# Attention blocks three half steps apart, silu of the gate ahead of the scan's end, first gate means earlier

## The reference, cut to what matters

```python
# 1  x += tanh(g0) * mamba(ctx, z=layernorm(x))
x = silu(conv(in_proj @ ctx) + b);  dt = softplus(dt_proj @ low(x) + b)
state = state * exp(dt * A[:, n]) + (dt * x) * B[n]      # n = 0..15, along 512 tokens
y = (sum_n state * C[n] + D * x) * silu(z)
# 2  x += tanh(.) * bitlinear(gelu(bitlinear(layernorm(x), w1)), w2)   ternary weights, 8 bit rows
# 3  attention = softmax(q @ k.T), q and k from ctx alone;  x += tanh(.) * layernorm(x) @ attention.T
# 4  x += tanh(.) * (gelu(layernorm(x) @ p1 + b1) @ p2 + b2)            512 to 2048 to 512
```

## Time and profile before

| | |
|---|---|
| median of 3 runs | 1008.52 us |
| the profiled execution | 1010.51 us, span 1008.7 us |
| busy: PE, DVE, ACT, POOL | 823.4, 806.3, 684.1, 560.5 us |
| granted clock of TensorE, mean | 0.91 |
| scans end (last product, DVE) | 168, 396, 614 and 833 us |
| tail on PE | 915.1 to 1003.3 us |

### The profile page before, as it was taken

One profiled execution on the slowest core, in us unless ns is written; L12 is line 12 of the kernel. 1 busy time (PEld: TensorE's weight loads), 2 busy tenths in 40 slices (PEclk: granted clock), 3 DMA queues, 4 the chain that ended last, 5 costly groups with the idle time before them and its releaser, 6 DMA issues. The chain is left out here.

```text
span 1008.7 us, 9403 instructions
## 1 busy us (share of the span) xinstructions
PE 823.4 (82%) x2758; PEld 405.3 (40%) x2798; DVE 806.3 (80%) x937; ACT 684.1 (68%) x1004; POOL 560.5 (56%) x477
## 2 busy tenths in 40 slices
PE   6531244699699998899699989898799989898998
PEld 2210012344344444444344434444343434446887
DVE  4989986686999998887999997977999997653333
ACT  4678985877389975575599863765699855624442
POOL 0398795123798984233998882225998871232000
PEclk9755556798999999999999999999999999998999
DMA  8078994000179987111199966301499972200331
GB/s 289 0 134 191 268 210 94 1 1 3 41 156 233 228 197 187 52 54 42 29 198 239 236 135 166 105 1 42 87 220 212 226 153 84 105 1 22 104 105 63
DMA packets 47971, 123.76 MB, mean 123 GB/s; under 512 B 5920, under 2 KB 7072, under 8 KB 47408
## 3 DMA queue, kind: packets, MB, share of 16 engines
q0 software_dynamic: 17280, 62.92, 33.1%
q1 hardware_dynamic: 30640, 60.24, 17.9%
HBM read 56.03 MB, written 4.19 MB: 60 GB/s over the span
## 5 line engine op out<-in xcount | busy, mean ns | idle before, releaser
L1686 POOL TENSOR_TENSOR work<-du,bcast 128x1024 f32<-128x1024 f32 x128 | 358.4, 2859 | 43.5 <-ACT ccast L857 37.7
L1258 DVE TENSOR_TENSOR_SCAN pair<-pair,work 128x512 f32<-128x512 f32 x256 | 299.2, 1214 | 18.5 <-ACT pair L872 13.7
L872 ACT ACTIVATE pair<-dt,a_neg 128x512 f32<-128x512 f32 x256 | 165.7, 680 | 47.6 <-DVE work L1263 39.3
L642 PE MATMUL bank<-stage,ring 128*128 128x512 f32 x384 | 172.9, 593 | 2.5 <-ACT stage L1101 2.0
L1263 DVE TENSOR_TENSOR work<-pair,ccast 128x1024 f32<-128x1024 f32 x128 | 156.8, 1225 | 12.8 <-DVE pair L1258 0.5
L1697 POOL DMA_DIRECT2D u<-work x120 | 138.5, 1157 | 43.7 <-DMA u<-work 21.9
L435 PE MATMUL bank<-xd,pick 128*128 128x512 bf16 x108 | 48.1, 446 | 95.9 <-ACT bcast L857 70.2
L642 PEld LDWEIGHTS bank<-stage,ring 128*128 128x128 f32 x384 | 71.8, 190 | 80.9 <-issue 70.9
L656 PE MATMUL bank<-ring,stage 128*128 128x512 f32 x192 | 86.1, 594 | 1.7 <-ACT hx L1136 1.7
L435 PEld LDWEIGHTS bank<-xd,pick 128*128 128x128 bf16 x128 | 12.9, 101 | 152.6 <-ACT bcast L857 104.2
L531 PE MATMUL pair<-w1q,qT 128*128 128x512 bf16 x247 | 59.8, 389 | 10.4 <-ACT qT L1079 6.7
(11 more groups left out here) (181 smaller groups left out, 1562.2 us busy)
## 6 DMA issues: line engine op xcount, KB each, us to landing
u<-work POOLq DMA_DIRECT2D x120, 512.0 KB, 6.0
ring<-ffn_dram SPq DMA_DIRECT2D x120, 256.0 KB, 4.9
ring<-ffn_dram SPq DMA_DIRECT2D x16, 512.0 KB, 3.4
xres<-x_dram SPq DMA_DIRECT2D x4, 1024.0 KB, 5.4
stage<-w_dram SPq DMA_DIRECT2D x1, 4096.0 KB, 17.5
stage<-w_dram SPq DMA_DIRECT2D x4, 1024.0 KB, 8.1
out_dram<-stage SPq DMA_DIRECT2D x16, 256.0 KB, 2.1
ctxT<-ctxT_dram SPq DMA_DIRECT2D x4, 512.0 KB, 6.2
```

Source lines behind the costliest of these rows:

```text
L642: last = pe.matmul(banks[2 + f % 2][:], piece(b, f)[:, k * P:(k + 1) * P], xnT[:, k, :], start=k == 0, stop=k == J - 1)
L872: act.activation(pairs[s % DECAYBUFS][:, q, :], dt[:, p * HALF + q, :], ACT.Exp, scale=a_neg[:, p * HALF + q, n:n + 1]).then_inc(s_decay, 1)
L1258: dve.tensor_tensor_scan(pair[:, q, :], pair[:, q, :], rows[:, q, :], 0.0, ALU.mult, ALU.add).then_inc(s_scan, 1)
L1686: pool.tensor_tensor(work[:, s % SCANBUFS, :, :], du[:, p * HALF:(p + 1) * HALF, :], bcast[:, n % 2, :].unsqueeze(1).broadcast_to([P, HALF ...
```

## The change

The attention's slots become steps of the scan: block j has its product, maximum and exponentials at half step 19 + 3j, reciprocal and scaling one later, transposes and copy one later still. The last block is then copied at half step 30, and nothing of the attention is left behind the scan. DVE's reciprocal moves in between the two scans of a half step and its product. `FFN_DOWN` now has 14 pairs in slots 9 to 12 (eight of round 0, six of round 1) instead of 13; the one more is the pair with which the turning began.

For batch 0, the gate means move to slot 6, and the weight steps on ACT are dealt out again: four instead of six are left behind the scan. POOL's part for w2 (`weight_rms(1)`) moves from slot 11 to slot 10.

In `turning`, `first_turning`, `between` and `closing` a few steps change places, and `closing` has two new rows of eight matmuls ahead of the tail.

```diff
-ATT_SLOTS = {9: 0, 10: 1, 11: 2, 12: 3}
+ATT_FIRST, ATT_EVERY = 18, 3
+ZSTAT_FIRST = 6
-W_MEAN = {6: 0, 11: 1}
+W_MEAN = {6: 0, 10: 1}
...
-W_LATE = (("scale", 1, 1), ("sign", 1, 1), ("scale", 1, 2), ("sign", 1, 2), ("scale", 1, 3), ("sign", 1, 3))
+W_LATE = (("scale", 1, 2), ("sign", 1, 2), ("scale", 1, 3), ("sign", 1, 3))
...
+def att_step(slot, which, p, step):
+    n = state_at(slot, which)
+    if n is None or 2 * n + p < ATT_FIRST + step:
+        return None
+    j, rest = divmod(2 * n + p - ATT_FIRST - step, ATT_EVERY)
+    return j if rest == 0 and j < J else None
@@ PE
+            def attention(b, slot, which, p):
+                done = att_step(slot, which, p, ATT_EVERY)
+                if done is not None:
+                    att_transpose(b, done)
+                j = att_step(slot, which, p, 1)
+                if j is not None:
+                    energies(b, j)
...
             def first_turning(m):
-                keep_awake(16)
+                keep_awake(24)
                 gate_transposes(m, (0, 1, 2, 3))
...
             def turning(b, m):
-                f_pair(b, 1, 10)
                 gate_transposes(m, (0,))
                 gate_transposes(m, (1,))
+                f_pair(b, 1, 12)
                 gate_transposes(m, (2,))
-                f_pair(b, 1, 12)
                 f_pair(b, 1, 14)
...
                 q_transposes(m, (2,))
+                up1(m, 1, (FC - 1,))
                 q_transposes(m, (3,))
-                up1(m, 1, (FC - 1,))
@@ between
+                transpose_h(b, 1)
                 down1(b, 0)
-                transpose_h(b, 1)
...
-                scan_bcast(m, 0, 0)
                 attend(b, 0)
                 attend(b, 1, m)
+                scan_bcast(m, 0, 0)
@@ closing
                 attend(b, 0)
+                down1(b, 3)
                 norm_transpose(b, 2)
-                down1(b, 3)
                 attend(b, 1)
+                norm_transpose(b, 3)
                 attend(b, 2)
-                norm_transpose(b, 3)
...
                 norm_transpose(b, 6)
+                keep_awake(8, 0)
                 norm_transpose(b, 7)
+                keep_awake(8, 0)
                 tail(b)
@@ ACT
                 gelu1(m, 1, range(FC - 1))
                 q_copy(m, (2,))
+                gelu1(m, 1, (FC - 1,))
                 q_copy(m, (3,))
-                gelu1(m, 1, (FC - 1,))
...
                     if slot == ZS_SLOT:
                         gates_silu(m)
-                att_copy(m, prev, J - 1)
@@ DVE
                     dve.tensor_tensor_scan(...)
+                if summed is not None:
+                    energy_sum(b, summed)
...
             def first_turning(m):
                 first_sum(m, 0)
                 first_sum(m, 1)
-                first_sum(m, 2)
                 q_norm(m, 0)
                 q_norm(m, 1)
                 q_out(m, 0)
+                first_sum(m, 2)
...
             def turning(b, m):
                 last_sum(m, 0)
+                last_sum(m, 1)
                 gated(m, 0)
-                last_sum(m, 1)
                 gated(m, 1)
@@ DVE, closing
-                weight_low(0)
-                weight_low(1)
                 norm_apply(b, 4)
                 third(b, 1)
+                weight_low(0)
                 third(b, 2)
+                weight_low(1)
```

More of the change, by code:

```diff
@@ L463, in project, with keep_awake @@
                 last.then_inc(s_inproj, 1)
-            def keep_awake(n):
+            def keep_awake(n, bank=3):
                 for k in range(n):
-                    pe.matmul(banks[3][:], identb[:], identb[:, None, :].broadcast_to([P, J, P]), start=True, stop=True)
+                    pe.matmul(banks[bank][:], identb[:], identb[:, None, :].broadcast_to([P, J, P]), start=True, stop=True)
             def low_rank(b):
@@ L794, in pass_ @@
                         keep_awake(16)
-                    if slot in ATT_SLOTS and ATT_SLOTS[slot]:
-                        att_transpose(m, ATT_SLOTS[slot] - 1)
+                    attention(m, slot, 0, 0)
                     if slot == QK_SLOT:
@@ L803, in pass_ @@
                     bcast_next(m, slot, 0, 1)
-                    if slot in ATT_SLOTS:
-                        energies(m, ATT_SLOTS[slot])
+                    attention(m, slot, 0, 1)
                     if slot == QK_SLOT:
@@ L813, in pass_ @@
                     bcast_next(m, slot, 1, 0)
+                    attention(m, slot, 1, 0)
                     if rest:
@@ L816, in pass_ @@
                     bcast_next(m, slot, 1, 1)
+                    attention(m, slot, 1, 1)
                     if rest:
                         f_unit(b, slot, 3)
-                if not rest:
-                    keep_awake(12)
-                att_transpose(m, J - 1)
                 if rest:
@@ L1058, in gate_squares, with attention @@
                                accum_out=zst[:, j, 2:3]).then_inc(s_zst, 1)
+            def attention(b, prev, slot, which, p):
+                done = att_step(slot, which, p, ATT_EVERY)
+                if done is not None:
+                    att_copy(b, prev, done)
+                j = att_step(slot, which, p, 1)
+                if j is not None:
+                    energy_exp(b, j)
+                j = att_step(slot, which, p, 2)
+                if j is not None:
+                    energy_probs(b, j)
             def quarter(b, slot, i, rest):
-                if slot == ZSTAT_SLOT - 1:
+                if slot == (ZSTAT_SLOT - 1 if rest else ZSTAT_FIRST):
                     gate_sum(b, i)
-                if slot == ZSTAT_SLOT:
+                if slot == (ZSTAT_SLOT if rest else ZSTAT_FIRST):
                     gate_mean(b, i)
@@ L1156, in pass_ @@
                     quarter(m, slot, 0, rest)
-                    if slot in ATT_SLOTS and ATT_SLOTS[slot]:
-                        att_copy(m, prev, ATT_SLOTS[slot] - 1)
+                    attention(m, prev, slot, 0, 0)
                     if slot == QK_SLOT:
@@ L1166, in pass_ @@
                     quarter(m, slot, 1, rest)
-                    if slot in ATT_SLOTS:
-                        energy_exp(m, ATT_SLOTS[slot])
+                    attention(m, prev, slot, 0, 1)
                     if slot == QK_SLOT:
@@ L1178, in pass_ @@
                     quarter(m, slot, 2, rest)
+                    attention(m, prev, slot, 1, 0)
                     decays(m, prev, slot, 1, 1)
@@ L1181, in pass_ @@
                     quarter(m, slot, 3, rest)
-                    if slot in ATT_SLOTS:
-                        energy_probs(m, ATT_SLOTS[slot])
+                    attention(m, prev, slot, 1, 1)
                     if rest:
@@ L1404, in half, with energy_max @@
                 if state_at(slot, which) is not None:
-                    half_step(b, state_at(slot, which), p)
-            def energy_max(b, slot):
-                if slot in ATT_SLOTS:
-                    j = ATT_SLOTS[slot]
+                    half_step(b, state_at(slot, which), p, att_step(slot, which, p, 2))
+                    energy_max(b, att_step(slot, which, p, 1))
+            def energy_max(b, j):
+                if j is not None:
                     dve.wait_ge(s_emm, b * J + j + 1)
@@ L1598, in pass_ @@
                     half(m, prev, slot, 0, 1)
-                    energy_max(m, slot)
                     if rest and (slot, 0) in FOURTH_SLOTS:
@@ L1602, in pass_ @@
                     half(m, prev, slot, 1, 0)
-                    if slot in ATT_SLOTS:
-                        energy_sum(m, slot)
                     half(m, prev, slot, 1, 1)
@@ L1797, in pass_ @@
                         bias(b, 3)
+                    if not rest:
+                        weights(slot)
                     half(m, prev, slot, 0, 1)
@@ L1800, in pass_ @@
                         bias(b, 1)
-                    if not rest:
-                        weights(slot)
                     half(m, prev, slot, 1, 0)
```

21 lines of the change are left out of this document (10 added, 11 removed).

## The result

The changed kernel takes 993.9 us (median of 4 runs, 993.35 to 998.15) against 1008.3 of the kernel before on the same chip (4 runs), ratio 0.9865, 95% interval 0.983 to 0.9899. Measured again with the experiments it takes 996.9 (5 runs, 994.24 to 999.54) against 1009.5, ratio 0.9873 (0.9851 to 0.9896). So it is faster by 13 to 14 us where 21.2 were forecast; 987.3 was too low, and the direction right. The median of its nine runs is 995.4. The profiled execution took 994.38 us, its span 992.6 (1008.7 before), mean granted clock 0.921. The spans differ by 16.1 us and the medians by 14.4, since the profiled execution of the kernel before (1010.51) was 2.2 above its median.

A forecast was written before the change was run, and what follows sets the result against it. DVE was taken to bound the kernel up to the tail at 915 us, with PE's chain close behind at the turnings. Terms 8.1 + 6.4 + 3.4 + 0.4 + 2.9 = 21.2 us off 1008.52 gave 987.3, 8-in-10 range 980 to 1000.

The forecast's parts named there:

- The turnings: Ends of the three scans beside layer 4: both DVE's and PE's chains shorten, 2.7 us per pass, 8.1 in three.
- the second begins at 399.3: In the turning, DVE's second sum waits for the last accumulating DMA, issued at 391.71 and landing 7.6 us later.
- PE's 403.0: In the turning, PE is through its pairs and transposes at 403.0 us, where before it was 405.8.
- PE's clock in the turnings: A product in the middle of PE's old 3.36 us wait keeps the clock up: 2.0 us of PE's gain.
- The first scan: First scan's end and turning: scan ends 2.3 us later, quantised transposes at 185.3 against 191.6; gain 6.4 us, bounds 3 and 9.
- The POOL cost: First scan: `weight_rms(1)`, 2.3 us, now stands ahead of five of POOL's inputs, so the scan ends 2.3 us later.
- The gelu: Behind each turning, DVE's wait for the second token block's gelu goes: 1.2 us each, 3.4 us in all, bounds 1 and 3.8.
- Closing and tail: `down1(b, 3)` comes earlier, 0.4 us; new rows of eight keep the clock up for the tail's first 24 matmuls, 2.9 us.
- the slower one: Rival: DVE's maximum inside the scan waits for PE, one pair behind, and the scan with it; 1018 us, 5%.
- the first one: Rival: the clock still falls at the three waits and the tail, PE holds the turnings; 995.9 us, 18%.
- the second rival: Rival: the first scan gives nothing back because of POOL, DMA and ACT's steps; 993.7 us, 10%.
- the silu was in time: Denies a rival: silu still late behind ACT's last decay and copy, or PE's pairs end as before; about 1007 us, 5%.

The follow-up runs named there:

- e3: Changed kernel with VectorE's old order in the later turnings (first sum, first gating, second sum, second gating): 991.0 us, ratio 0.9822.
- e2: Changed kernel with GpSimd's block of gate means one slot later in passes 1 to 3: 991.6 us, ratio 0.9811.
- e4: Changed kernel with the moved gelu step undone, again behind the last transposes and copies: 999.2 us, ratio 0.9897.
- e7: Changed kernel with one more row of seven small matmuls in the closing, ahead of down1(0): 994.1 us, ratio 0.9844.
- e6: Changed kernel with GpSimd's gate-mean block of the first batch behind slot 8 instead of 10: 991.1 us, ratio 0.9813.
- the control: The changed kernel run again with no edit, beside the experiments: 996.9 us, ratio 0.9873 to the kernel before.
- e10: e9_both with a full row of 128 x 512 between the step-size products between passes: 993.9 us, ratio 0.9827.
- e9_both: Changed kernel with the old sum and gating order, GpSimd's gate means behind slot 11 (passes 1 to 3) and 8 (pass 0): 987.0 us.
- e11_both_no_tail_rows: e9_both without the closing's two rows of eight matmuls: 986.3 us, ratio 0.9756.

## Why the prediction came out as it did

The direction and the places were right, the size was not: the sum was 21.2 us, the profiled executions differ by 16.1 and the medians by 14.4. In the traces the turnings gave 3.6 us less than forecast, the closing 2.5 and the gelu 1.0 less, the first scan 0.8 more, and 1.1 came from the start. By its terms:

- **The turnings, 8.1 forecast, 4.5 measured** (B 6.4 less 1.9 in the scans). This is the term that was most off, and the step in it is "the second begins at 399.3", the accumulating DMA's landing. Forecast was 3.0 us behind the scan's end; it landed 4.0, 4.4 and 4.1 behind. The old time was kept, and of what it rests on one half held: the GpSimd queue's way from its block of small steps to the next issue is the same (9.7 us behind the product before it, in the first two of these turnings, before and after), and the maximum lengthens the scan by 0.6. But the last issue waits for the landing of the DMA before it in its half, and that one took 7.3 and 7.5 us in these two turnings instead of 6.2. Why it took longer is not isolated; while the first of them was under way SyncE's queue moved 1.01 MB in 7.3 us, and in the kernel before 0.62 MB in 6.2. With the second sum 1.1 us late, both gatings behind it were late and PE's 403.0 was not the bound. The old order of sums and gatings would have hidden 0.9 to 1.2 us of that (e3), and earlier DMAs hide it all (e2). The prediction has the gating as work behind the sum and doesn't ask whether it could stand in the wait. With both mended B is 7.3, which is 3.4 less than before and 2.7 net of the scan, the forecast's figure. It then ends on PE, whose transposes are ready 6.8 us behind the scan's end (392.4 against 385.6); 6.7 were forecast (403.0 against 396.3).
- **PE's clock in the turnings**: right. The granted clock is 1.00 in the three later turnings of every trace but that of the kernel before, with the product in the middle of the wait. No run took the product out, so that it is what holds the clock is argued.
- **The first scan, 6.4**: A gave 7.2, right in size and partly by luck. Up to the first quantised rows, where the forecast was read, it is 5.6 (144.8 us behind the scan's first product before, 139.2 after); the rest is a second wait for the scaling, ahead of the third row block, that fell from 3.39 to 0.34 us and that the prediction doesn't name. It is 1.4 to 1.8 in e2, e4 and e7, so this part changes with the execution. The POOL cost (2.3 forecast) is 2.6 in the scan, DVE's wait 3.69 instead of 2.50, and e6 takes it back by moving the gate means' block and not `weight_rms(1)`, to which the prediction put it.
- **The gelu, 3.4**: some 3, right. C as a whole gave only 2.4, since the clock fell for longer in the stretch after pass 2 (69.2; down1(3) at 6.38 us, 5.31 before).
- **Closing and tail, 3.3**: 0.8 in the first profile, 2.4 in the control (148.4 to 146.0). The tail's first 24 matmuls came down as forecast (8.58 to 5.73 us), but the versions without the rows have half of that too (7.09 and 7.31), so only half is shown to be theirs. In the first profile 1.6 went back to down1(0), whose clock fell, at a place that the prediction doesn't name.
- **The rivals**: no maximum in the scan waits for PE in passes 1 to 3, so the slower one is out. The clock didn't fall at the three turnings nor at the tail, so the first one didn't happen either. The clock does fall between the passes, but there it fell in the kernel before too. The first scan gave back its term, so the second rival is out, and the silu was in time. That 993.9 lies at the second rival's price (993.7) and near the first's (995.9) is chance: neither is what the traces show.

## What to carry to other kernels

When a wait goes, list all that the same instruction waits for and price the next one by its own release, back to the instruction that starts that chain; read the waits in the kernel beside the releaser that a timeline names, which can be another that ended at the same time. An instruction that needs only the first of two results belongs in the wait for the second. Small steps on a queue that also issues transfers cost twice, once for its own work and once for what lands late. A gain that rests on TensorE's clock is to be counted from several executions, and a filler row belongs where a trace shows an idle gap, not where PE is busy.

## What the runs showed of the hardware

- Twelve steps of one element per partition hold GpSimd's queue from 153.46 to 158.89 us, 0.19 to 0.56 each, with gaps of 0.21 between dependent ones: about twice the time of one of its products of 128x1024 around them (2.65 to 3.30 us).
- The last four accumulating DMAs of 512 KB of the second scan landed 5.3, 7.3, 8.0 and 7.5 us after their issue in the changed kernel, where the first three were issued 3 us apart, and 4.6, 4.7, 5.3 and 6.5 in e2, where they were issued 3.6 to 4.9 apart.
- TensorE's granted clock fell to 0.50 with PE busy 2.00 of 2.00 us (450 to 452 us in e10), from a stretch with products 16 rows deep on. It fell there or at down1(3) behind them in 26 of the 39 stretches of column C outside e10. In 8 of them down1(3) took 5.5 to 6.4 us. e9_both has the fall in all three stretches and e11_both_no_tail_rows, with the same instructions there, in none.
- Gaps of 0.80 and 1.63 us ahead of down1(0) are followed by 3.61 us in one execution and 5.17 in another of the same kernel.
